# A recommender tower on one core: row transposes and MLP products at the array's full width, and part of ScalarE's copies one step sooner

## The chip, the cores and the metric

The kernel runs on one core of a Trainium2 chip. The metric is device time in microseconds (us), from the start of the program to the end of its last instruction. A change counts here as measurable when it is over 1% of the time, about 12 us.

TensorE is written PE in the profile, its weight loads PEld, VectorE DVE, ScalarE ACT, GpSimd POOL, and SyncE, which issues most plain DMAs, SP. On this kernel's float32 operands every matmul of the code appears in the trace as two records of MATMUL and two of LDWEIGHTS; a bfloat16 matmul appears as one of each. A record of MATMUL with its LDWEIGHTS is called a pair below.

## The reference

For a batch of 2048, 40 categorical fields are looked up in 40 tables with rows of 32 floats. Every pair of fields (780 pairs) gives one bilinear number; these and 16 dense values go through an MLP:

```python
e = jnp.stack([tbl_0[ids[:, 0]], ..., tbl_39[ids[:, 39]]], axis=1)      # (2048, 40, 32)
z = jnp.einsum('bpd,pde,bpe->bp', e[:, iidx, :], bilinear_matrices, e[:, jidx, :])   # (2048, 780)
h = jnp.concatenate([z, dense_ctx], axis=1)                             # (2048, 796)
h = jnp.maximum(h @ W_top1 + b_top1, 0.0)                               # 512 wide
h = jnp.maximum(h @ W_top2 + b_top2, 0.0)                               # 256 wide
y = h @ W_top3                                                          # (2048, 1)
```

## The kernel before

**Tiling.** The batch is cut into five blocks `o` of 256, 512, 512, 512 and 256 rows (`ROWS`). The 40 fields are ten chunks `J` of four fields, so that a chunk's vectors, transposed, fill 128 partitions (`x_T`, `x_look`: partition = field and dimension, column = batch row). A unit `(a, J)` stands for the field pairs between chunks a and J; 50 units cover everything. Where `a` is even, the unit `(a, a)` also takes the pairs inside chunk a + 1; it is the twin unit, and it needs the tile `x_twin`, a reordered mixture of chunk a + 1 and chunk a. Chunks are worked from 9 down to 0, so units are few at the start of a block and many (ten for chunk 0) at its end. A cycle `g` is one unit of 512 rows, or two units of 256 rows; there are 200 cycles: 25, 50, 50, 50 and 25.

**Where the vectors come from.** Seven fields (36 to 39, 0, 2, 3) are looked up on TensorE: VectorE compares indices (`one_hot`, L599) and TensorE multiplies ones with the table in three bfloat16 parts (`look`, L682). The other 33 fields are gathered by GpSimd: `DMA_INDIRECT` at L425, 128 rows each, 528 in all. A chunk's gathers go to one of 12 slots of `rows`. A turn (`turn`, L705) transposes a slot's rows: one matmul with the identity for each 128 rows and each field, which writes 32 partitions of a bank of `U`; ScalarE copies that bank to `x_T` (`keep_turn`, L467). Before GpSimd may fill the slots for turn n it waits for turn n - 12 (`turned`). Turns come in the order of chunks, so they are 2, 2, 4, 4, 6, 6, 8 cycles apart in a block of 512 rows.

**A cycle.** TensorE's program is one list written out by the loop at the end: `project(g + 1)` (L733, and L742 for a twin unit), which multiplies x with the bilinear matrices to `U`; then `sum_up(g - 1)` (L758), which adds VectorE's products over partitions into `bank_z`; then the cycle's parts of looks or of the MLP from the table `MISC_AT` (L682 or L788); then any turn. VectorE multiplies `U` by the other chunk (`multiply`, L617 to L635). ScalarE's list follows the same cycles: `keep_z` (L456), `keep_look`, `keep_mlp` (L503, L506), `keep_turn` (L467), then `copy_twin` (L491, L494, L496), seven copies in three lines, the last of which signals `twin_copied`; TensorE waits for it before a twin unit.

**The MLP.** A job `("mlp", o, j)` is one result tile of 128 rows of h1 (j = 0 to 3, seven parts t each), of h2 (j = 4, 5, four parts) or y (j = 6). A part before the change is four matmuls, each with 32 columns of weights, which fill the four quarters of one bank. The last block's MLP stands behind the loop: `sum_up(G - 1)`, then for each t the four j of h1, then h2 and y.

In the trace's names 128*32 stands for a weight tile of 128 partitions by 32 columns.

## Time and profile before

| what | value |
|---|---|
| median of 3 runs | 1256.24 us (1253.74 to 1262.59) |
| the profiled execution's own time | 1248.72 us |
| its span in the trace | 1247.1 us |
| mean granted clock of TensorE | 0.797 of full speed |
| TensorE busy, MATMUL records | 885.4 us (71%), 7918 |
| VectorE busy | 537.8 us (43%) |
| ScalarE busy | 176.0 us (14%) |
| GpSimd busy | 505.1 us (41%), 528 gathers of 955 ns |

The table is read so: TensorE is the busiest engine, but is idle or held up for over a quarter of the span, and most of that lies in the first two thirds. The profiled execution is 7.5 us below the median.

### The profile page before, as it was taken

The numbers are of one execution on the slowest core, as the hardware profiler recorded it, in microseconds if no ns is written. First come the engines' busy times: TensorE is split into PE (matmuls) and PEld (weight loads), VectorE is DVE, ScalarE is ACT, GpSimd is POOL, SyncE is SP. The second block draws the span as 40 slices with busy tenths as digits, with TensorE's granted clock in tenths as the row PEclk, the third lists the DMA queues.
The fourth block names the chain that finished last, engine by engine and source line by source line (L and its number), as shares of the span: only waits on it lengthen the run. The fifth ranks groups of instructions, "written<-read, shape, count | busy, mean of one in ns | idle before, by whom it ended". The sixth has DMA issues, their size and how long they took to land.

```text
span 1247.1 us, 18181 instructions
## 1 busy us (share of the span) xinstructions
PE 885.4 (71%) x7918; PEld 317.4 (25%) x7918; DVE 537.8 (43%) x601; ACT 176.0 (14%) x318; POOL 505.1 (41%) x535
## 2 busy tenths in 40 slices
PE   3110034668767668797897865699997889999998
PEld 2000011224322222222232221122223222324444
DVE  3000012226434233464475323276663558776652
ACT  2000111010101201020110210102112112024121
POOL 7777556662444565524431564612315430000000
PEclk8555555767767777797798777889997889999999
DMA  4200000361122100100010010000000000000000
GB/s 77 38 13 13 11 10 11 48 70 18 33 53 38 18 12 11 23 6 9 9 13 5 10 13 9 13 4 6 6 4 11 9 6 2 1 1 2 2 2 2
DMA packets 61280, 20.04 MB, mean 16 GB/s; under 512 B 46759, under 2 KB 60396, under 8 KB 61202
## 3 DMA queue, kind: packets, MB, share of 16 engines
q0 software_dynamic: 16896, 8.68, 5.2%
q1 hardware_dynamic: 44292, 10.18, 4.5%
q8 instruction: 62, 1.02, 0.3%
q14 instruction: 16, 0.13, 0.0%
q10 hardware_dynamic: 14, 0.03, 0.0%
HBM read 18.81 MB, written 0.04 MB: 15 GB/s over the span
## 4 chain that ended last, share of the span: by engine, by line
PE 61%; another core or an unknown queue 21%; issue 12%; ACT 4%; DVE 1%; DMA 0%; ACTq 0%; DVEq 0%
PE U L733 19%; PE bank_z L758 18%; PE misc L788 10%; PE misc L682 5%; PE U L705 4%; PE U L742 3%; ACT x_twin L491 1%; PE U L788 1%; DVE prod L635 1%; ACT x_twin L494 1%; ACT x_twin L496 0%; ACT x_T L467 0%; ACT z L456 0%; ACT W L529 0%
## 5 line engine op out<-in xcount | busy, mean ns | idle before, releaser
L425 POOL DMA_INDIRECT rows<-in_tbl,idx x528 | 504.3, 955 | 522.9 <-PE U L705 349.0
L635 DVE TENSOR_TENSOR prod<-U,x_T 128x1024 f32<-128x1024 f32 (+1 forms) x308 | 343.0, 1149 | 242.9 <-PE U L733 118.2
L733 PE MATMUL U<-x_T,W 32*128 32x512 f32 (+1 forms) x1440 | 245.7, 598 | 133.9 <-ACT x_twin L496 73.1
L758 PE MATMUL bank_z<-prod,select 128*32 128x512 f32 (+1 forms) x2000 | 272.6, 572 | 52.6 <-issue 40.7
L635 DVE TENSOR_TENSOR prod<-U,x_look 128x1024 f32<-128x1024 f32 (+1 forms) x90 | 89.1, 1007 | 240.1 <-PE U L742 101.0
L733 PEld LDWEIGHTS U<-x_T,W 32*128 32x128 f32 x1440 | 89.2, 201 | 263.1 <-issue 197.0
L682 PE MATMUL misc<-ones,tabs 125*32 125x512 bf16 (+1 forms) x1050 | 97.9, 390 | 61.0 <-issue 59.1
L788 PE MATMUL misc<-z,W 128*32 128x512 f32 (+1 forms) x952 | 117.1, 569 | 6.5 <-issue 5.5
L599 DVE TENSOR_SCALAR ones<-idx_wide,row_of 125x2048 bf16<-125x2048 f16 (+3 forms) x100 | 58.4, 606 | 134.3 <-remote 93.5
L705 PE MATMUL U<-ident,rows 128*32 128x128 f32 x1056 | 65.9, 305 | 68.8 <-issue 68.6
L758 PEld LDWEIGHTS bank_z<-prod,select 128*32 128x32 f32 x2000 | 53.4, 113 | 238.8 <-issue 167.0
L682 PEld LDWEIGHTS misc<-ones,tabs 125*32 125x32 bf16 x1050 | 42.5, 107 | 124.8 <-issue 109.3
L467 ACT ACTIVATE x_T<-U 128x512 f32<-128x512 f32 (+1 forms) x40 | 20.5, 512 | 378.6 <-PE U L705 325.5
L705 PEld LDWEIGHTS U<-ident,rows 128*32 128x32 f32 x1056 | 44.4, 123 | 106.1 <-issue 103.4
L733 PE MATMUL U<-x_look,W 32*128 32x512 f32 (+1 forms) x360 | 51.8, 565 | 3.7 <-issue 2.1
L456 ACT ACTIVATE z<-bank_z 128x512 f32<-128x512 f32 (+1 forms) x35 | 17.9, 512 | 254.9 <-remote 144.5
L788 PEld LDWEIGHTS misc<-z,W 128*32 128x32 f32 x952 | 33.6, 117 | 71.3 <-issue 63.7
L742 PE MATMUL U<-x_twin,W 32*64 32x512 f32 (+1 forms) x200 | 44.4, 604 | 2.1 <-issue 2.0
L788 PE MATMUL misc<-h,W 128*32 128x512 f32 (+3 forms) x272 | 39.7, 572 | 6.5 <-issue 3.1
L491 ACT ACTIVATE x_twin<-x_T 32x512 f32<-32x512 f32 (+1 forms) x80 | 43.4, 542 | 1.8
L742 PE MATMUL U<-x_T,W 32*64 32x512 f32 (+1 forms) x160 | 35.3, 605 | 3.9 <-ACT x_twin L496 3.0
L617 DVE TENSOR_TENSOR prod<-U,x_T 128x512 f32<-128x512 f32 (+1 forms) x20 | 11.6, 581 | 46.7 <-PE U L742 24.5
(64 smaller groups left out, 242.4 us busy)
## 6 DMA issues: line engine op xcount, KB each, us to landing
rows<-in_tbl,idx POOLq DMA_INDIRECT x528
idx_wide<-idx_rows SPq DMA_DIRECT2D x3, 500.0 KB
idx_wide<-idx_rows SPq DMA_DIRECT2D x3, 375.0 KB
W<-in_W_top SPq DMA_DIRECT2D x35, 2.0 KB
W<-_L_rec_bilinear_matrices SPq DMA_DIRECT2D x4, 128.0 KB
W<-in_W_top SPq DMA_DIRECT2D x1, 512.0 KB
W<-_L_rec_bilinear_matrices SPq DMA_DIRECT2D x30, 4.0 KB
W<-in_W_top SPq DMA_DIRECT2D x8, 56.0 KB
```

The lines of the kernel that those rows point to most:

```text
L425: nc.gpsimd.indirect_dma_start(out=rows[:, n % R_SLOTS, t, f, :], out_offset=None, in_=tables[field][:, :], in_offset=bass.IndirectOffsetO ...
L456: nc.scalar.activation(z[:, at % Z_SLOTS, 0:ROWS[o]], bank_z[:, 0:ROWS[o]], ACT.Copy).then_inc(z_kept, 1)
L467: nc.scalar.activation(x_of(o, J)[lo:hi, :], U[lo:hi, at, 0:N], ACT.Copy).then_inc(turn_kept, 1)
L491: nc.scalar.activation(x_twin[r * DIM:(r + 1) * DIM, 1, 0:N], x_of(o, a + 1)[(CF - 1 - r) * DIM:(CF - r) * DIM, :], ACT.Copy)
L599: nc.vector.tensor_scalar(ones[:, n % ONES, 0:len(fs), 0:N], idx_wide[q][:, :, 0:N], row_of[0:KP, k:k + 1], None, ALU.is_equal).then_inc(o ...
L635: last = nc.vector.tensor_tensor(to[:, :, m * N:(m + n) * N].rearrange("p r (m n) -> p r m n", m=n), U[:, at:at + 2, m * N:(m + n) * N].re ...
L682: last = nc.tensor.matmul(misc[f * DIM:(f + 1) * DIM, 0:N], tabs[0:KP, LOOKED.index(field), part, k * DIM:(k + 1) * DIM], ones[:, n % ONES ...
L705: last = nc.tensor.matmul(U[f * DIM:(f + 1) * DIM, at, t * P:(t + 1) * P], rows[:, n % R_SLOTS, t, f, :], ident[:], start=True, stop=True, ...
L733: last = nc.tensor.matmul(U[:, at + r % 2, m * N:(m + 1) * N], W[row, at_W:at_W + P], x_of(o, a)[row, :], start=True, stop=True, skip_grou ...
L742: last = nc.tensor.matmul(U[side * P // 2:(side + 1) * P // 2, at + r % 2, m * N:(m + 1) * N], W[row, at_W + side * P // 2:at_W + (side + ...
L758: last = nc.tensor.matmul(bank_z[r * DIM:(r + 1) * DIM, 0:N], sel, prod[:, (2 * g + r // 2) % P_SLOTS, r % 2, m * N:(m + 1) * N], start=(k ...
L788: last = nc.tensor.matmul(res, lhs, rhs, start=(t == 0), stop=(t == depth - 1), skip_group_check=True)
```

## The change

1. **Turns.** Where all four fields of a chunk are gathered (eight of the nine turns of a block), each 128 rows are turned by one `transpose` of 128x128 in place of four matmuls with 32 columns of weights. The turn of chunk 0, with one gathered field, is as before.
2. **MLP.** A part of h1 or h2 is one matmul with 128 columns of weights in place of four with 32. y is as before.
3. **ScalarE's copies.** `copy_twin` is cut in two. Six of its seven copies, which read chunk a + 1 alone, stand in ScalarE's list as soon as that chunk is there and the last twin unit has been multiplied (`TWIN_AT`); the seventh, which reads chunk a, stands where all seven stood (`mix_twin`, `MIX_AT`).
4. **Closing MLP.** Of the last block's h1, the six parts t < 6 of j = 0 come ahead of the last `sum_up`, then the six parts of j = 1, 2, 3, then the four last parts.

```diff
+    _mix = max(turn_cycle(_o, _a), TWIN_CYCLE[_n] - 3)
+    MIX_AT[_mix].append(_n)
+    TWIN_AT[min(_mix, max(turn_cycle(_o, _a + 1), TWIN_CYCLE[_n - 1] + 1 if _n else -2))].append(_n)
...
+            def mix_twin(n):
+                (o, a), N = TWINS[n], ROWS[TWINS[n][0]]
+                wait_kept(o, a)
                 nc.scalar.activation(x_twin[2 * DIM:, 0, 0:N], x_of(o, a)[2 * DIM:, :], ACT.Copy
                                      ).then_inc(twin_copied, 1)
...
                 for t in range(ROWS[o] // P):
-                    for f in GATHERED[c]:
-                        last = nc.tensor.matmul(U[f * DIM:(f + 1) * DIM, at, t * P:(t + 1) * P],
-                                                rows[:, n % R_SLOTS, t, f, :], ident[:], start=True, stop=True,
-                                                skip_group_check=True)
+                    if len(GATHERED[c]) == CF:
+                        last = nc.tensor.transpose(U[:, at, t * P:(t + 1) * P],
+                                                   rows[:, n % R_SLOTS, t].rearrange("p f d -> p (f d)"), ident[:])
+                    else:
...
-                for q in range(CF if j < RESULTS - 1 else 1):
-                    if j < H1 // P:
-                        lhs = W1[:, t, j * P + q * DIM:j * P + (q + 1) * DIM]
...
-                    res = bank[q * DIM:(q + 1) * DIM, 0:N] if j < RESULTS - 1 else bank[0:1, 0:N]
+                if j < H1 // P:
+                    lhs, rhs = W1[:, t, j * P:(j + 1) * P], z[:, (o * ZT + t) % Z_SLOTS, 0:N]
...
+                res = bank[:, 0:N] if j < RESULTS - 1 else bank[0:1, 0:N]
...
-            sum_up(G - 1)
             o, n = BLOCKS - 1, JOB[("mlp", BLOCKS - 1, 0)]
             pe.wait_ge(misc_kept, n)
-            for t in range(ZT):
-                for j in range(H1 // P):
-                    mlp(o, j, t, misc if j == 0 else U[:, j - 1, :])
+            for t in range(ZT - 1):
+                mlp(o, 0, t, misc)
+            sum_up(G - 1)
+            for j in range(1, H1 // P):
+                for t in range(ZT - 1):
+                    mlp(o, j, t, U[:, j - 1, :])
+            for j in range(H1 // P):
+                mlp(o, j, ZT - 1, misc if j == 0 else U[:, j - 1, :])
```

On TensorE, at the start of block 2 (a turn, a twin unit with the close of block 1's sums, and the first MLP parts), the program before reads (a row is an operation, its tiles, the output's size and the count of matmuls in the code):

```order
310 L705 MATMUL U<-ident,rows 32x128 x16
311 L742 MATMUL U<-x_T,W 64x512 x2
...
317 L758 MATMUL bank_z<-prod,select 32x512 x4
318 L766 MATMUL bank_z<-ident,dense 32x128 x16
319 L788 MATMUL misc<-z,W 32x512 x4
320 L733 MATMUL U<-x_T,W 128x512 x4
```

and after:

```order
310 L722 MATMUL U<-ident,rows 128x128 x4
311 L763 MATMUL U<-x_T,W 64x512 x2
...
317 L779 MATMUL bank_z<-prod,select 32x512 x4
318 L787 MATMUL bank_z<-ident,dense 32x128 x16
319 L806 MATMUL misc<-z,W 128x512
320 L754 MATMUL U<-x_T,W 128x512 x4
```

Nothing has moved there; sixteen instructions have become four, and four have become one.

On ScalarE, at the twin unit of chunk 0 in block 3, before (with the semaphores waited for; L467 is the copy behind chunk 0's turn):

```order
179 L503 ACTIVATE h1<-misc,b1 128x512 [waits mlp_full]
180 L467 ACTIVATE x_look<-U 32x512 [waits turned]
181 L491 ACTIVATE x_twin<-x_T 32x512 [waits misc_kept,turn_kept,multiplied]
182 L491 ACTIVATE x_twin<-x_T 32x512 x3
183 L494 ACTIVATE x_twin<-x_T 32x512 x2
184 L496 ACTIVATE x_twin<-x_look 64x512
```

and after:

```order
180 L501 ACTIVATE x_twin<-x_T 32x512 [waits turn_kept,multiplied]
181 L501 ACTIVATE x_twin<-x_T 32x512 x3
182 L504 ACTIVATE x_twin<-x_T 32x512 x2
183 L518 ACTIVATE h1<-misc,b1 128x512 [waits mlp_full]
184 L475 ACTIVATE x_look<-U 32x512 [waits turned]
185 L511 ACTIVATE x_twin<-x_look 64x512 [waits misc_kept,turn_kept]
```

Six copies have moved ahead of an MLP copy and of the turn's copy; one is left behind the turn.

On TensorE at the program's end, before:

```order
774 L758 MATMUL bank_z<-prod,select 32x256 x16
775 L766 MATMUL bank_z<-ident,dense 32x128 x8
776 L788 MATMUL misc<-z,W 32x256 x4
777 L788 MATMUL U<-z,W 32x256 x12
```

and after:

```order
774 L779 MATMUL bank_z<-prod,select 32x256 x8
775 L806 MATMUL misc<-z,W 128x256 x6
776 L779 MATMUL bank_z<-prod,select 32x256 x8
777 L787 MATMUL bank_z<-ident,dense 32x128 x8
778 L806 MATMUL U<-z,W 128x256 x18
779 L806 MATMUL misc<-z,W 128x256
780 L806 MATMUL U<-z,W 128x256 x3
```

Six MLP parts now stand between the last two sums; the rest of h1 follows them, result by result.

## Rows read from the trace of the kernel before

**Rows 1.** The page: busy time of each engine, and slices of GpSimd
```profile
PE 885.4 (71%) x7918; PEld 317.4 (25%) x7918; DVE 537.8 (43%) x601; ACT 176.0 (14%) x318; POOL 505.1 (41%) x535
...
POOL 7777556662444565524431564612315430000000
```

**Rows 2.** Windows, core 0: busy us and records of PE, PEld, DVE, ACT, POOL; clock
```profile
15.00:148.00 133.00, 15.29 (x78) 5.07 (x78) 3.99 (x11) 4.96 (x5) 100.79 (x106) 0.52 0.16 25
164.00:184.00 20.00, 8.13 (x64) 3.81 (x68) 3.97 (x7) 3.44 (x9) 15.34 (x16) 0.50 0.09 14
184.00:204.00 20.00, 5.12 (x28) 1.37 (x17) 1.29 (x2) 0.00 (x0) 15.14 (x16) 0.59 0.10 13
...
564.00:574.00 10.00, 9.21 (x90) 3.17 (x90) 5.48 (x6) 0.60 (x1) 7.56 (x8) 1.00 0.09 13
574.00:584.00 10.00, 4.77 (x15) 1.73 (x17) 1.23 (x1) 0.00 (x0) 7.57 (x8) 0.65 0.11 13
...
936.00:962.00 26.00, 19.46 (x149) 6.70 (x152) 9.40 (x9) 6.78 (x11) 15.14 (x16) 0.82 0.10 12
...
1056.00:1066.00 10.00, 10.00 (x84) 2.63 (x80) 8.04 (x8) 4.55 (x8) 0.00 (x0) 1.00 0.01 2
```

**Rows 3.** Timeline of POOL: first gather of a burst, and what ended its wait
```profile
690.29 0.95 POOL L425 DMA_INDIRECT rows<-in_tbl,idx  x1 [28.29 <-PE U L705]
...
738.14 0.94 POOL L425 DMA_INDIRECT rows<-in_tbl,idx  x1 [5.17 <-PE U L705]
...
792.58 0.95 POOL L425 DMA_INDIRECT rows<-in_tbl,idx  x1 [3.73 <-PE U L705]
825.50 0.95 POOL L425 DMA_INDIRECT rows<-in_tbl,idx  x1 [13.20 <-PE U L705]
```

**Rows 4.** Waits in all: us, times, longest us
```profile
POOL rows L425 <- PE U L705: 349.0, 29, 28.3
PE U L742 <- ACT x_twin L496: 11.7, 5, 3.8
```

**Rows 5.** Timeline of PE in block 3, no gathers under way
```profile
1087.11 1.14 PE L733 MATMUL U<-x_T,W 32*128 32x512 f32 x8
1088.18 1.07 PE L758 MATMUL bank_z<-prod,select 128*32 128x512 f32 x8
1089.06 1.04 PE L788 MATMUL misc<-h,W 128*32 128x512 f32 x8
1089.93 1.04 PE L705 MATMUL U<-ident,rows 128*32 128x128 f32 x8
```

**Rows 6.** Timeline of PE: a full turn of 512 rows; two MLP parts
```profile
562.91 1.05 PE L705 MATMUL U<-ident,rows 128*32 128x128 f32 x32
...
1145.63 1.90 PE L788 MATMUL misc<-z,W 128*32 128x512 f32 x16
1147.35 0.62 PE L705 MATMUL U<-ident,rows 128*32 128x128 f32 x16
```

**Rows 7.** Timeline of ACT and PE at the twin unit of chunk 0, block 3
```profile
1091.00 0.59 ACT L467 ACTIVATE x_look<-U 32x512 f32<-32x512 f32 x1 [8.50 <-PE U L705]
1091.67 2.54 ACT L491 ACTIVATE x_twin<-x_T 32x512 f32<-32x512 f32 x4
...
1095.50 0.63 ACT L496 ACTIVATE x_twin<-x_look 64x512 f32<-64x512 f32 x1
...
1096.38 0.65 PE L742 MATMUL U<-x_look,W 32*64 32x512 f32 x2 [2.49 <-ACT x_twin L496]
```

**Rows 8.** The chain that ended last, a turn inside a burst of gathers: start, us
```profile
730.84 0.21 PE U L705 x2
...
736.00 1.86 PE U L705 x26
```

**Rows 9.** Timeline at the start: ACT and POOL
```profile
138.55 0.38 ACT L476 ACTIVATE x_look<-misc 128x256 f32<-128x256 f32 x1 [123.85 <-remote]
...
163.78 0.38 ACT L467 ACTIVATE x_T<-U 128x256 f32<-128x256 f32 x1 [20.27 <-remote]
```

More of the change, by code:

```diff
@@ L198, with turn_cycle @@
 TWIN_AT = {g: [] for g in range(-2, G)}
+MIX_AT = {g: [] for g in range(-2, G)}
+def turn_cycle(o, J):
+    return next((g for g in TURN_AT if (o, CHUNK_OF_STEP.index(J)) in TURN_AT[g]), -2)
 for _n, (_o, _a) in enumerate(TWINS):
-    _turned = next(g for g in TURN_AT if (_o, CHUNK_OF_STEP.index(_a)) in TURN_AT[g])
-    TWIN_AT[max(_turned, TWIN_CYCLE[_n] - 3)].append(_n)
+    _mix = max(turn_cycle(_o, _a), TWIN_CYCLE[_n] - 3)
+    MIX_AT[_mix].append(_n)
+    TWIN_AT[min(_mix, max(turn_cycle(_o, _a + 1), TWIN_CYCLE[_n - 1] + 1 if _n else -2))].append(_n)
 U_SLOTS = 3
@@ L477, in keep_look, with wait_kept @@
                 last.then_inc(misc_kept, 1)
+            def wait_kept(o, J):
+                c = CHUNK_OF_STEP.index(J)
+                if GATHERED[c]:
+                    act.wait_ge(turn_kept, TURN[(o, c)] + 1)
+                if c in GROUP_OF_STEP:
+                    act.wait_ge(misc_kept, JOB[("look", o, GROUP_OF_STEP[c])] + 1)
             def copy_twin(n):
                 (o, a), N = TWINS[n], ROWS[TWINS[n][0]]
-                c = CHUNK_OF_STEP.index(a)
                 if n:
                     act.wait_ge(multiplied, 2 * (TWIN_CYCLE[n - 1] + 1))
-                for J in (a, a + 1):
-                    if GATHERED[CHUNK_OF_STEP.index(J)]:
-                        act.wait_ge(turn_kept, TURN[(o, CHUNK_OF_STEP.index(J))] + 1)
-                    if CHUNK_OF_STEP.index(J) in GROUP_OF_STEP:
-                        act.wait_ge(misc_kept, JOB[("look", o, GROUP_OF_STEP[CHUNK_OF_STEP.index(J)])] + 1)
+                wait_kept(o, a + 1)
                 for r in range(CF):
@@ L550, in _ @@
                     copy_twin(n)
+                for n in MIX_AT[g]:
+                    mix_twin(n)
             for j in range(RESULTS):
@@ L703, in turn @@
                 for t in range(ROWS[o] // P):
-                    for f in GATHERED[c]:
-                        last = nc.tensor.matmul(U[f * DIM:(f + 1) * DIM, at, t * P:(t + 1) * P],
-                                                rows[:, n % R_SLOTS, t, f, :], ident[:], start=True, stop=True,
-                                                skip_group_check=True)
+                    if len(GATHERED[c]) == CF:
+                        last = nc.tensor.transpose(U[:, at, t * P:(t + 1) * P],
+                                                   rows[:, n % R_SLOTS, t].rearrange("p f d -> p (f d)"), ident[:])
+                    else:
+                        for f in GATHERED[c]:
+                            last = nc.tensor.matmul(U[f * DIM:(f + 1) * DIM, at, t * P:(t + 1) * P],
+                                                    rows[:, n % R_SLOTS, t, f, :], ident[:], start=True, stop=True,
+                                                    skip_group_check=True)
                 last.then_inc(turned, 1)
@@ L776, in mlp @@
                     pe.wait_ge(z_kept, o * ZT + t + 1)
-                for q in range(CF if j < RESULTS - 1 else 1):
-                    if j < H1 // P:
-                        lhs = W1[:, t, j * P + q * DIM:j * P + (q + 1) * DIM]
-                        rhs = z[:, (o * ZT + t) % Z_SLOTS, 0:N]
-                    elif j < RESULTS - 1:
-                        m = j - H1 // P
-                        lhs = W2[:, t, m * P + q * DIM:m * P + (q + 1) * DIM]
-                        rhs = h1[:, t, 0:N]
-                    else:
-                        lhs, rhs = W3[:, t:t + 1], h2[:, t, 0:N]
-                    res = bank[q * DIM:(q + 1) * DIM, 0:N] if j < RESULTS - 1 else bank[0:1, 0:N]
-                    last = nc.tensor.matmul(res, lhs, rhs, start=(t == 0), stop=(t == depth - 1),
-                                            skip_group_check=True)
+                if j < H1 // P:
+                    lhs, rhs = W1[:, t, j * P:(j + 1) * P], z[:, (o * ZT + t) % Z_SLOTS, 0:N]
+                elif j < RESULTS - 1:
+                    m = j - H1 // P
+                    lhs, rhs = W2[:, t, m * P:(m + 1) * P], h1[:, t, 0:N]
+                else:
+                    lhs, rhs = W3[:, t:t + 1], h2[:, t, 0:N]
+                res = bank[:, 0:N] if j < RESULTS - 1 else bank[0:1, 0:N]
+                last = nc.tensor.matmul(res, lhs, rhs, start=(t == 0), stop=(t == depth - 1), skip_group_check=True)
                 if t == depth - 1:
```

## The prediction

> **What bounds the kernel now.** The page first: TensorE is busy for 71% of the span with 7918 pairs, GpSimd for 41% [rows 1]. GpSimd's slices show that its gathers run until about 1030 us, and the reader should see that they come in bursts. So I read TensorE in windows laid over those bursts. In 10 us without a gather TensorE passes 84 pairs; in the first 10 us of a burst 90, in the second 10 us of the same burst 15, with nothing but "issue" before them [rows 2]. Over a longer burst it is worse: 64 pairs in the first 20 us from 164 us on, 28 in the next 20, and 78 in the 133 us from 15 to 148 us [rows 2]. Something about a running burst holds TensorE up, after a number of pairs that varies much less than their time does. I call these stretches the crawl; the rows don't tell its cause. It seems to go by instructions: in a crawl a turn of 32 pairs takes from 730.8 to 737.9 us, where it takes 1.05 us otherwise [rows 6, 8].
>
> A burst ends when GpSimd meets a slot whose turn has not run: that wait is 349.0 us in all [rows 4], and it is also what lets TensorE recover. Turn n starts gathers of turn n + 12; so the two engines hand each other the time. GpSimd's own work, 528 gathers at 8 in 10 us [rows 2], is 660 us and isn't changed.
>
> From about 825 us on the bursts are short and the kernel is bound by TensorE: project 1.07 us, sum 0.88, MLP part 0.87, one behind the other [rows 5], while VectorE is busy for 8.04 of 10 us [rows 2].
>
> **Twin copies.** At chunk 0 the turn is followed by seven copies, 1091.67 to 1096.13 us, and TensorE starves for 2.49 us at the twin unit [rows 7]; there are 5 such waits with 11.7 us [rows 4]. Only the 0.59 us copy of the turn and the 0.63 us seventh copy stay behind the turn, so 3.8 us leave that path, about the longest of the five waits. At the startup twin both halves keep their place, so nothing is gained there. The six copies now queue ahead of an MLP copy; they wait for `multiplied` of a cycle whose sum ScalarE's next z copy awaits anyway, and what stands behind them on ScalarE is late by 3.8 us at most, with the MLP's next job behind it. That takes back some. Between -12 and 0; I take **-10**.
>
> **Turns, where TensorE runs freely.** 32 pairs take 1.05 us [rows 6]; these are four column tiles working side by side, so each of the eight passes of a tile takes about 0.12 us. The same follows from chunk 0's turn, whose 8 pairs in one tile take 1.04 us [rows 5]. No row shows a 128x128 transpose. If it still takes two passes, a turn of 512 rows is 8 passes one behind another, about 1 us, and nothing is gained; if it takes one, 0.5. Twenty-four turns of 512 rows and sixteen of 256 are changed: at the lower end 24 x 0.5 + 16 x 0.25 = 16 us less, at the other 0. Cycles that VectorE bounds hide some of it; I take **-12**, near the one-pass end, since a transpose moves data and need not be split like a product.
>
> **MLP parts, where TensorE runs freely.** Two parts of 512 rows take 1.72 us from 1145.63 to 1147.35 [rows 6], 0.86 each: 8 pairs in four tiles at once, so two passes of 0.43 us. One matmul of 128 columns also needs two passes over 512 columns, 0.86 us. So the streaming gives nothing back; fewer instructions do nothing here. What is new is a change of the array's shape between sum (32 columns wide) and part (full). Rows: project, whose shape differs from its neighbours', takes 1.07 us to the next start, the sum with the same four matmuls 0.88 [rows 5]. A change so costs 0 to 0.2 us, and 114 cycles hold a changed part: 0 to +23. I take 0.1 each, **+12**.
>
> The Trainium skill, TensorEngine Tiling, Key Properties, speaks against the change here: changing the tiling mode, and not just the tile, drains the engine. It gives no time; the 0.2 us above is the only price there is, and with it the sum would be 12 us higher.
>
> **Thinner instruction stream in the crawl.** A cycle of 512 rows is 8 + 8 + 8 pairs with an MLP part and becomes 18; a turn is 32 and becomes 4 or 8. Looks (9 or 12 pairs a part) stay, and fill most cycles until 435 us, and again from 489 to 710. If a burst passes about 90 pairs whatever they are, the work of a burst grows only where MLP parts and turns fall into it. Taken burst by burst from GpSimd's restarts [rows 3]:
> - 690.3 to 738.1 us (two turns, each two cycles behind the last): 73 + 120 pairs become 45 + 80. The first turn now ends within 7 us, so GpSimd doesn't stop: its 40 us run on to 730, the second 20 with hardly any progress, and the last 30 pairs need the time until about 738. Gain 0: the two bursts have joined.
> - 738.1 to 792.6: 120 + 128 pairs become 74 + 82; the same join, then rest: 788, gain 5.
> - 792.6 to 825.5: 168 become 110. 90 pass in the 22 us of the burst, 20 more at 8.4 a us: 25 us instead of 33, gain 8.
> - 458 to 690 us, five bursts filled mostly with looks: about 3.5 us in each of the two that hold MLP parts at their start, 7.
> - 850 to 990 us, bursts of 10 us, some of which meet: 936 to 962 us holds 149 pairs where 218 would pass at the free rate [rows 2], 8 us lost. Two or three such places, most of it given back: 10.
>
> Together **-30**; -5 if the crawl goes by time alone, -90 if joined bursts still passed 90 pairs per 20 us (below).
>
> **Startup and block 0.** The chain's 120 look pairs are done at 138.5 us, turn 0 at 163.8 [rows 9]: 16 pairs in 25 us, of which 2 or 4 remain, 14 to 20 us sooner. But GpSimd's first burst ends at 148 us; with turn 0 done by then it doesn't stop, and project(0), 24 pairs, falls into the crawl until turn 12's gathers end at 168 and TensorE has recovered (15 us after the first burst). Turn 1 then comes at about 187 in place of 181, turn 2 sooner (its burst no longer joined), turn 3 about where it was. I take **0**, between -15 and +20.
>
> **The close.** TensorE fills a gap of half a microsecond before the last sum; 36 parts stream as before. **-1**.
>
> **Sum.** -10 - 12 + 12 - 30 + 0 - 1 = -41: 1248.7 becomes about 1208 us for the profiled execution. The median lies 7.5 us above that execution; with the same distance the forecast is **1215 us**.
>
> **The rivals.**
> *The crawl admits pairs, not time, even in joined bursts.* Then the 23 full bursts each carry 90 of pairs that are 30% richer (7918 pairs become about 6000, 25% fewer, for nearly the same work): 23 x 90 x 0.3 / 8.4 = 74 us in place of 30, and startup gives its 15. 1215 - 44 - 15 = 1156 us. For it: the first halves of bursts. Against: 28 pairs in the second 20 us from 184 on, 78 in 133 us [rows 2]. 18%.
> *The crawl doesn't care for instructions, or full-width passes cost more.* Copies and turns gain 22, the crawl 5, and shape changes take 23: 1256 - 4 = 1252 us, no measurable change. 15%.
> *Joined bursts: slower.* Turns get done early, GpSimd never stops, and TensorE crawls for 40 us and more. A join costs the 90 pairs that a fresh burst would have passed less those it does pass; at 28 that is 62 pairs, 7 us. It can happen at startup, and at three places in each of blocks 1 and 2, where turns are two cycles apart: 7 x 7 = 49 us, where my sum counts them as quits. With the thinning reduced to 15 for it: 1215 + 49 + 15 = 1279 us. It decides if a join passes fewer than 30 pairs. Against it: GpSimd's work is finite, and a join moves its waits, which are 349 us [rows 4], to later, where there are no bursts. 10%.
> *The forecast itself*, 57%.
>
> **How the numbers follow.** My own case spans 1180 to 1240 us by the ends of its terms. The range of 8 in 10 runs from 1155, which takes in the large gain, to 1252, which takes in the case of no change. Measurement tells 1% or 12.6 us from no change: faster by more than that 0.77, within it 0.13, slower 0.10.
>
> **What would show it.** Turn records fall from 1056 to about 160 or 290 (one pass or two), MLP records by some 1080; waits on the seventh copy at a twin unit fall from 11.7 us to under 2. MLP cycles from 1030 to 1226 us stay at 2.9 to 3.0 us. Windows over bursts hold about 90 pairs, and more sums. GpSimd's restarts between 690 and 825 come less often but not sooner on the whole. The prediction is wrong if the crawl vanishes or lengthens, or if a full-width part takes over 1.1 us where it took 0.86.

## The result, and the profile of the kernel after

After: 1239.26 us median of 19 runs (1233.35 to 1253.81); before, on the same chips: 1256.78 us (1249.62 to 1264.24). The ratio is 0.987, 95% interval 0.985 to 0.990: some 17 us less, just over the 1% that counts here, where the forecast had 41 us less. Here and in the table below medians are of all runs, while ratios leave out the runs of a slower state (one of after's 19 here; two of e14's four). The profiled execution of after took 1244.90 us, its span is 1243.3 us, the mean granted clock 0.783.

The two profiled executions lie only 3.8 us apart (1248.72 and 1244.90): the one of before is faster than its median, the one of after slower. So the two traces can show what a burst or a cycle costs, but not where the whole 17 us lie.

The page of after: busy time of the engines, and slices of GpSimd.

```profile
PE 878.8 (71%) x5942; PEld 306.9 (25%) x5942; DVE 539.2 (43%) x601; ACT 175.5 (14%) x318; POOL 505.8 (41%) x535
...
POOL 7777647462445566514432646522224430000000
```

Against [rows 1], 1976 pairs are gone and TensorE's busy time is 6.6 us shorter: a quarter of the instructions was hardly any of the work.

Waits in all in after (us, times, longest); L722 and L726 are the turns (full, and chunk 0), L763 the twin unit, L754 a project.

```profile
POOL rows L433 <- PE U L722: 280.3, 22, 27.6
...
PE U L754 <- ACT x_twin L511: 92.1, 1, 92.1
...
POOL rows L433 <- PE U L726: 53.0, 3, 20.5
...
PE U L763 <- ACT x_twin L511: 1.2, 1, 1.2
```

GpSimd waits for turns 333 us where it waited 349, and the five waits at twin units with 11.7 us [rows 4] have become one with 1.2. The wait of 92.1 us is the startup's and no new one; before has it at L733 with 71.8 us.

Windows of after, columns as in [rows 2]: the startup burst, a joined burst in block 0, a joined burst at 690 us, a stretch without gathers.

```profile
15.00:148.00 133.00, 12.09 (x72) 3.71 (x65) 4.21 (x12) 1.93 (x5) 100.86 (x106) 0.51 0.16 25
...
186.30:206.30 20.00, 13.20 (x92) 5.57 (x92) 11.45 (x18) 4.56 (x11) 15.39 (x16) 0.67 0.09 14
206.30:226.70 20.40, 6.37 (x11) 1.92 (x12) 0.00 (x0) 0.00 (x0) 15.48 (x17) 0.50 0.09 13
...
688.60:708.60 20.00, 13.01 (x85) 3.66 (x81) 6.45 (x7) 2.90 (x6) 15.10 (x17) 0.73 0.08 12
708.60:728.30 19.70, 3.16 (x9) 1.15 (x9) 1.23 (x1) 0.00 (x0) 15.09 (x16) 0.50 0.09 13
1056.00:1066.00 10.00, 10.00 (x74) 2.89 (x74) 7.13 (x7) 0.60 (x1) 0.00 (x0) 1.00 0.01 2
```

The crawl is unchanged: some 80 to 90 pairs at the front of a burst, then almost nothing. Bursts join at 186 and at 690 us, as forecast, and at 941 us. The join forecast at 738 us didn't come: GpSimd waited 3.3 us at 764.22.

GpSimd's restarts in after, to set beside [rows 3].

```profile
688.62 0.94 POOL L433 DMA_INDIRECT rows<-in_tbl,idx  x1 [27.53 <-PE U L722]
...
741.26 0.94 POOL L433 DMA_INDIRECT rows<-in_tbl,idx  x1 [13.00 <-PE U L722]
...
764.22 0.94 POOL L433 DMA_INDIRECT rows<-in_tbl,idx  x1 [3.31 <-remote]
...
792.29 0.94 POOL L433 DMA_INDIRECT rows<-in_tbl,idx  x1 [8.40 <-PE U L722]
826.91 0.94 POOL L433 DMA_INDIRECT rows<-in_tbl,idx  x1 [14.94 <-PE U L722]
```

This is the reading that matters. 690.29, 738.14, 792.58 and 825.50 us of before are 688.62, 741.26, 792.29 and 826.91: where the forecast had TensorE gain 13 us from 690 to 825 us, it has lost 3. Other traces with the crawl, from several chips, bear that out. Times between the starts of the same gathers (numbered from 0; the last column is from gather 510 to the end of the span), in us:

| trace | 378 to 458 (690 to 825 us in before) | 442 to 458 (the last burst of these) | 262 to 378 | 462 to 510 | 510 to the end |
|---|---|---|---|---|---|
| before | 135.2 | 32.9 | 255.5 | 140.8 | 262.2 |
| e7, before's code but for the start | 135.1 | 33.8 | 265.6 | 140.7 | 262.7 |
| e8, turns alone | 139.1 | 33.5 | 265.1 | 139.7 | 262.7 |
| e13, copies alone | 139.0 | 33.6 | 263.8 | 140.9 | 253.6 |
| e9, MLP alone | 134.9 | 34.8 | 256.0 | 135.3 | 271.1 |
| after | 138.3 | 34.6 | 255.5 | 138.8 | 258.8 |

From 378 to 458 no thinner stream gains anything; in the last of these bursts the two kernels with the 128-wide MLP parts are 1 to 2 us slower than the four others, where 8 us were to be won. From 262 to 378 (about 435 to 690 us) the same code differs by 10 us between before and e7, so single traces settle nothing there.

### What one burst does with the thinner stream

Both kernels start a burst at 792 us; the last gather is issued at 811. TensorE in after, then in before.

```profile
801.95 1.99 PE L754 MATMUL U<-x_T,W 32*128 32x512 f32 x8
803.88 1.06 PE L779 MATMUL bank_z<-prod,select 128*32 128x512 f32 x8
805.65 1.13 PE L754 MATMUL U<-x_T,W 32*128 32x512 f32 x4 [0.71 <-issue]
816.19 2.07 PE L754 MATMUL U<-x_T,W 32*128 32x512 f32 x4 [9.41 <-DVE prod L652]
818.19 1.94 PE L779 MATMUL bank_z<-prod,select 128*32 128x512 f32 x8
820.06 2.08 PE L806 MATMUL misc<-z,W 128*128 128x512 f32 x2
822.07 2.08 PE L754 MATMUL U<-x_T,W 32*128 32x512 f32 x8
824.08 1.06 PE L779 MATMUL bank_z<-prod,select 128*32 128x512 f32 x8
```

```profile
805.10 1.12 PE L733 MATMUL U<-x_T,W 32*128 32x512 f32 x2
806.65 1.01 PE L733 MATMUL U<-x_T,W 32*128 32x512 f32 x2 [0.43 <-issue]
813.69 2.08 PE L733 MATMUL U<-x_T,W 32*128 32x512 f32 x4 [6.03 <-issue]
815.70 1.94 PE L758 MATMUL bank_z<-prod,select 128*32 128x512 f32 x8
817.56 1.98 PE L733 MATMUL U<-x_T,W 32*128 32x512 f32 x8
819.47 1.06 PE L758 MATMUL bank_z<-prod,select 128*32 128x512 f32 x8
```

Both stall at 806 us in the middle of a project, but after is one project and one sum further on: behind the stall it has one more project until the turn, before has two. Priced by rows at the free rate, that lead is worth about 1.5 us (6.1 us of work up to the turn instead of 7.7). Then after comes out of the stall at 816.2 instead of 813.7, and four of its groups instead of three take about twice their time (2.08 against 1.14 us for a whole project): they run at the lower of the clock's two levels, 1.2 GHz (granted clock 0.50 from 816.2 to 824.0 us, 0.51 from 813.7 to 819.4 us in before), after 9.41 us of idle time where before had 6.03. They lose 3.7 us by it, before's three 2.8. So 2.5 and 0.9 us are lost against 1.5 won, and the turn starts 1.9 us later (826.03 for 824.14).

The stall is not TensorE's alone. VectorE in after, then in before:

```profile
814.91 4.70 DVE L652 TENSOR_TENSOR prod<-U,x_T 128x1024 f32<-128x1024 f32 x4 [9.32 <-remote]
```

```profile
812.41 1.23 DVE L635 TENSOR_TENSOR prod<-U,x_T 128x1024 f32<-128x1024 f32 x1 [11.49 <-remote]
```

In after VectorE sat idle for 9.32 us, though the last matmul of the half project that it multiplies had begun at 802.49 us; TensorE's 9.41 us are a wait for VectorE in turn. In before that matmul began at 800.10 us and the multiplication at 812.41. In free cycles it follows after about 1 us. So inside the crawl TensorE's work is also made known late, or finished late (the ends of matmuls are modelled), and the forecast's "nothing but issue" is half of the picture. In e3's trace, which has no crawl, VectorE sits idle for over 1 us beyond that first microsecond at 2 of its 400 multiplications; in after's trace at 42.

### A cycle that nothing disturbs

TensorE in after, block 3.

```profile
1081.29 1.13 PE L806 MATMUL misc<-h,W 128*128 128x512 f32 x2
1082.35 1.14 PE L754 MATMUL U<-x_T,W 32*128 32x512 f32 x8
1083.42 1.06 PE L779 MATMUL bank_z<-prod,select 128*32 128x512 f32 x8
1084.41 1.12 PE L806 MATMUL misc<-h,W 128*128 128x512 f32 x2
```

And in before, the part ahead of [rows 5]:

```profile
1086.14 1.04 PE L788 MATMUL misc<-h,W 128*32 128x512 f32 x8
```

From part to part 3.12 us, in before 2.92. In before the sum is followed after 0.88 us [rows 5], here after 0.99, and the part after 1.06 where one with 32 columns takes 0.97 to the next project (1087.11). So it is 0.1 us at each of the two borders, 0.2 us a cycle: the forecast had charged 0.1 a cycle.

### The profile page after: what moved, and what is told of

Its sections match the earlier page's. It is cut to its first block, busy times and chain, and to the rows that moved or that the text cites. A ratio compares the mean times of both kernels' runs of the same rounds, so it can differ in the third digit from the quotient of the medians.

```text
span 1243.3 us, 14228 instructions
## 1 busy us (share of the span) xinstructions
PE 878.8 (71%) x5942; PEld 306.9 (25%) x5942; DVE 539.2 (43%) x601; ACT 175.5 (14%) x318; POOL 505.8 (41%) x535
## 4 chain that ended last, share of the span: by engine, by line
PE 58%; another core or an unknown queue 27%; issue 10%; ACT 3%; DVE 1%; DMA 0%; ACTq 0%; DVEq 0%
PE U L754 18%; PE bank_z L779 17%; PE misc L806 11%; PE misc L699 6%; PE U L763 3%; PE bank_z L787 1%; PE U L722 1%; PE U L806 1%; DVE prod L652 1%; ACT x_twin L501 1%; ACT x_T L475 0%; ACT z L464 0%; PE U L726 0%; ACT x_twin L504 0%
## 5 line engine op out<-in xcount | busy, mean ns | idle before, releaser
L754 PE MATMUL U<-x_T,W 32*128 32x512 f32 (+1 forms) x1440 | 238.2, 599 | 166.6 <-ACT x_twin L511 92.1
L779 PE MATMUL bank_z<-prod,select 128*32 128x512 f32 (+1 forms) x2000 | 264.9, 568 | 42.5 <-issue 24.9
L754 PEld LDWEIGHTS U<-x_T,W 32*128 32x128 f32 x1440 | 88.2, 202 | 285.4 <-issue 208.9
L699 PE MATMUL misc<-ones,tabs 125*32 125x512 bf16 (+1 forms) x1050 | 107.9, 401 | 66.8 <-issue 64.0
L806 PE MATMUL misc<-z,W 128*128 128x512 f32 (+1 forms) x238 | 121.4, 612 | 3.4 <-ACT h L518 3.4
L806 PEld LDWEIGHTS misc<-z,W 128*128 128x128 f32 x238 | 40.5, 202 | 82.3 <-issue 75.9
L754 PE MATMUL U<-x_look,W 32*128 32x512 f32 (+1 forms) x360 | 52.6, 574 | 3.9 <-DVE prod L652 3.6
L763 PE MATMUL U<-x_T,W 32*64 32x512 f32 (+1 forms) x160 | 40.0, 634 | 14.0 <-DVE prod L652 10.3
L806 PE MATMUL misc<-h,W 128*128 128x512 f32 (+3 forms) x80 | 39.9, 593 | 8.0 <-ACT x_look L482 6.4
L787 PE MATMUL bank_z<-ident,dense 128*32 128x128 f32 x128 | 18.3, 332 | 35.6 <-issue 35.6
L763 PE MATMUL U<-x_twin,W 32*64 32x512 f32 (+1 forms) x200 | 40.8, 614 | 1.0 <-issue 0.9
L640 DVE TENSOR_TENSOR prod<-U,x_twin 128x1024 f32<-128x1024 f32 (+1 forms) x25 | 25.1, 1004 | 21.9 <-remote 21.9
L722 PE MATMUL U<-ident,rows 128*128 128x128 f32 x128 | 24.5, 298 | 9.8 <-issue 9.7
```

Source lines behind the costliest of these rows:

```text
L640: last = nc.vector.tensor_tensor(to[:, :, m * N:(m + 1) * N], U[:, at:at + 2, m * N:(m + 1) * N], x_twin[:, :, 0:N], ALU.mult)
L699: last = nc.tensor.matmul(misc[f * DIM:(f + 1) * DIM, 0:N], tabs[0:KP, LOOKED.index(field), part, k * DIM:(k + 1) * DIM], ones[:, n % ONES ...
L722: last = nc.tensor.transpose(U[:, at, t * P:(t + 1) * P], rows[:, n % R_SLOTS, t].rearrange("p f d -> p (f d)"), ident[:])
L754: last = nc.tensor.matmul(U[:, at + r % 2, m * N:(m + 1) * N], W[row, at_W:at_W + P], x_of(o, a)[row, :], start=True, stop=True, skip_grou ...
L763: last = nc.tensor.matmul(U[side * P // 2:(side + 1) * P // 2, at + r % 2, m * N:(m + 1) * N], W[row, at_W + side * P // 2:at_W + (side + ...
L779: last = nc.tensor.matmul(bank_z[r * DIM:(r + 1) * DIM, 0:N], sel, prod[:, (2 * g + r // 2) % P_SLOTS, r % 2, m * N:(m + 1) * N], start=(k ...
```

## Experiments

The same kernel has two conditions that no text of it chooses. The kernel before took 1256 to 1274 us in three of the five sets of runs, as in the recorded result, and **774 us in the two others**; within a set it was always the same, and one chip (number 6) showed 774 in the first set and 1274 ten minutes later. The forecast was made for the slow one. Each kernel is compared with before in its own set.

| run | kernel | before, us | this, us | ratio (95% interval) |
|---|---|---|---|---|
| e1 | turns alone | 773.7 | 772.9 | 0.999 (0.998 to 1.000) |
| e2 | MLP alone | 773.7 | 782.5 | 1.013 (1.011 to 1.015) |
| e3 | copies alone | 773.7 | 768.4 | 0.993 (0.991 to 0.995) |
| e4 | after without the MLP's part | 773.7 | 766.3 | 0.991 (0.989 to 0.993) |
| e5 | after | 1273.7 | 1251.9 | 0.980 (0.975 to 0.986) |
| e6 | before, pause after 8 gathers | 1273.7 | 1185.9 | 0.929 (0.924 to 0.935) |
| e7 | before, pause for the first look | 1273.7 | 1267.9 | 0.997 (0.994 to 1.000) |
| e8 | turns alone | 1256.2 | 1261.5 | 1.001 (0.998 to 1.004) |
| e9 | MLP alone | 1256.2 | 1257.3 | 1.001 (0.998 to 1.005) |
| e10 | after, pause after 8 | 1256.2 | 1114.5 | 0.886 (0.880 to 0.891) |
| e11 | e4's kernel, pause after 8 | 1256.2 | 1118.1 | 0.887 (0.882 to 0.892) |
| e12 | before, probes on GpSimd | 1270.7 | 1300.0 | one run |
| e13 | copies alone | 1270.7 | 1263.5 | 0.994 (0.991 to 0.997) |
| e14 | after, pause after 6 | 1270.7 | 945.6 | 0.735 (0.728 to 0.741) |
| e15 | after, pause after 4 | 1270.7 | 957.9 | 0.755 (0.751 to 0.758) |
| e16 | before, pause after 6 | 774.0 | 895.7 | 1.157 (1.154 to 1.159) |
| e17 | e4's kernel, pause after 6 | 774.0 | 888.5 | 1.147 (1.145 to 1.149) |
| e18 | e4's kernel, pause after 5 | 774.0 | 906.0 | 1.172 (1.169 to 1.176) |

### The parts alone (e1 to e4)

Each is the kernel before with one hunk of the change's diff: e1 `nc.tensor.transpose` in `turn`, e2 the single matmul in `mlp`, e3 `mix_twin` and its table; e4 has all but e2's.

> The kernel before with the 128x128 transposes alone. In the kernel after, a turn of 512 rows takes some 0.5 us where it took 1.05, and turns 3 to 26 end within a few us of where they ended before. Theory (the gain of the turns lies only where TensorE runs freely, and GpSimd's bursts swallow the rest): about 6 to 16 us faster than before, 1240 to 1250 us. Rival (the thinner stream helps within a burst, and the MLP's change took it back): 25 us or more, 1230 or less.

> The kernel before with the MLP parts as 128x128 matmuls alone. The trace of after shows an MLP cycle at 3.12 us where it was 2.93, that is 0.2 us for each of 114 cycles, 81 of them past 900 us. Theory (two changes of the array's shape cost 0.1 us each, and nothing in the bursts pays for it): 10 to 20 us slower than before, 1266 to 1276 us. Rival, the recorded forecast's terms: 12 us for the shapes, less the MLP's share of the thinner stream, some 15 us: no change, 1253. A third: the 0.2 us belong to the turns' and copies' side of the change, and this kernel is within 3 us of before with cycles at 2.93.

> The kernel before with ScalarE's six copies made sooner, alone. Waits of TensorE on x_twin outside of the startup fell from 11.7 to 1.2 us in after. Theory: 5 to 10 us faster, 1246 to 1251 us. Rival (the work behind a twin unit only waits for VectorE instead): within 3 us of before.

> The kernel after with the MLP parts as in before (32 columns of weights): transposes, copies and the closing order stay. Theory (the MLP's part of the change costs 10 to 20 us): 1220 to 1230 us, faster than after's 1239. Rival (thinner MLP parts help in the bursts as much as they cost elsewhere): 1237 to 1241, as after.

No crawl was there. The page of e3, busy times and slices of TensorE and GpSimd:

```profile
PE 688.5 (90%) x7918; PEld 269.2 (35%) x7918; DVE 532.8 (69%) x601; ACT 175.7 (23%) x318; POOL 510.1 (67%) x535
...
PE   4579999677799999986999999996999999999998
...
POOL 7777777777777777777777777777777777700000
```

GpSimd gathers in one burst from 3 to 672 us, TensorE is 90% busy beside it with the same 7918 pairs, and nobody slows anybody. So the bound is different: GpSimd's list until 672 us, TensorE's 95 us after it. In that regime the parts read cleanly. The MLP costs 8.8 us, and all of it falls in the last 50 cycles, at 0.2 us each (49 x 0.2 = 10); at 610 us e1 and e2 are level within 1 us. The copies give 5.3 us. The turns give 0.8, within the noise. e4's 7.4 is the copies', the turns' and about one for the close. The theory for e3 held; e2 cost a little less than the 10 to 20 us expected, and for e1 less came than the 6 to 16 us, since GpSimd hides what is won before 672 us. All four were meant for the condition with the crawl, so for it they say nothing yet.

### After again, and a pause between gathers (e5 to e7)

e6 and all later kernels with a pause:

```diff
+            issued, left = [0] * R_SLOTS, 8
             for n, (o, c) in enumerate(TURNS):
...
                         ).then_inc(gathered[n % R_SLOTS], 16)
+                        issued[n % R_SLOTS] += 1
+                        left -= 1
+                        if left == 0:
+                            pool.wait_ge(gathered[n % R_SLOTS], 16 * issued[n % R_SLOTS])
+                            left = 8
```

e7 has `if n == 1: pool.wait_ge(ones_used, KC)` there instead.

> The kernel after, unchanged, beside before on the chip of this call. On the chip of the first four comparisons before took 773.7 us and had no crawl: GpSimd gathered without a stop to 672 us and TensorE was never held up. If this call's chip is like that one: the parts there were -0.8 (turns), -5.3 (copies), +8.8 (MLP), and -7.4 for all but the MLP; theory, they add up: +1 to +3 us, 774 to 777. Rival (the closing order and the faster turns hide part of the MLP's cost): 770 or less. If it is like the chip of the recorded result (before near 1256 us): 0.987 of before again.

> The kernel before, with GpSimd waiting after every eighth gather until those of that slot have landed, about 2.5 us: 66 pauses. Theory (the crawl is made by an unbroken run of gathers, and a short pause ends it): on a chip where before takes some 1256 us, 850 to 1000 us. Rival (the crawl goes by the number of gathers or by something else on that chip): 1250 us or more. On a chip where before takes 774 us there is nothing to cure and GpSimd is the bound: 66 pauses of 2.3 us cost 100 to 155 us, 875 to 930 us.

> The kernel before, with GpSimd waiting after turn 0's eight gathers until TensorE has done the first look (ten parts). Theory, on a chip with the crawl: the look takes 20 us in place of 125, the remaining 106 gathers run from about 40 to 172 us, beside work of block 0 instead of the look: 30 to 100 us faster than 1256. Rival (the crawl falls on block 0's cycles instead): within 12 us. On a chip without the crawl the gathers are GpSimd's bound and all come some 20 us later: 790 to 800 us.

e5 repeats the result and is, at 0.980 (0.975 to 0.986), a little better. e6 took 88 us off a kernel by making GpSimd wait: the pause theory is right in sign and too bold in size (850 to 1000 us were expected, 1186 came). e7 fits its rival: the copy behind turn 0 began at 23 us in place of 164, but the 138 gathers behind the look still ran in one burst, from 18 to 190 us, and the copy behind turn 2 began at 212 us where before has 210. The burst has to be broken, not moved.

### The parts with the crawl (e8, e9, e13)

> The transposes alone again, for the condition with the crawl (before at 1256 to 1274 us). Before against after by the ends of the turns showed no gain up to 900 us, though a turn of 512 rows has 8 pairs in place of 32. Theory (the bursts swallow the thinner stream; some 6 us come from turns past 900 us): 0.990 to 0.998 of before. Rival (the transposes do thin the crawl and the MLP's change hid it): 0.98 or less. In the condition without the crawl (before at 774 us): 0.999 again.

> The 128-wide MLP parts alone again, for the condition with the crawl. Without the crawl they cost 0.2 us in each cycle of the last 50, where TensorE is the bound, and nothing before, where GpSimd is. With the crawl TensorE is the bound in 81 such cycles from about 900 us on: theory, 16 us, and 6 parts' worth fewer records in the bursts of blocks 1 and 2 give back 0 to 10: 1.005 to 1.013 of before. Rival, the recorded forecast (12 us for shapes, 15 us back from the thinner stream): 0.998. In the condition without the crawl: 1.013 again.

> ScalarE's six copies made sooner, alone, for the condition with the crawl (before 1256 us). Turns alone and MLP alone gave 1.001 each there, and all together 0.980 to 0.987. Theory (the copies carry most of the gain): 0.985 to 0.993. Rival (the parts gain only together, as when turns and copies move in the same bursts): 0.997 to 1.003. Without the crawl: 0.993 again.

Alone, turns and MLP are each worth nothing (1.001), the copies 8 us (4 to 12). e8 so missed both of its texts (0.998 at most was expected), e9 came out between its theory and its rival, and e13 at the edge of its theory. Three parts make 5 us less, give or take about 7 by their intervals; the whole change made 16 us less by the recorded ratio and 25 by e5's. The rest, 10 to 20 us, comes only in combination or from the closing order, which was not tried alone; for the latter the traces show nothing (from the z copy to the end 20.6 us in after, 20.7 in before). These are different sets of runs, so some of the rest can be a difference between sets.

Within the MLP's 1.5 us two things cancel. From gather 510 to the end, where the bursts are nearly over, e9's trace is 8.9 us longer than before's (271.1 for 262.2, table above): the borders' price. From 462 to 510 it is 5.5 us shorter (135.3 for 140.8): there the thinner MLP parts do gain.

Why the turns give nothing even late, e8's TensorE at a turn of 256 rows between two MLP parts and a project:

```profile
1159.13 1.90 PE L792 MATMUL misc<-z,W 128*32 128x512 f32 x16
1160.96 0.44 PE L705 MATMUL U<-ident,rows 128*128 128x128 f32 x2
1161.33 1.16 PE L737 MATMUL U<-x_T,W 32*128 32x256 f32 x16
```

and before's project behind the same turn as in [rows 6]:

```profile
1147.90 1.16 PE L733 MATMUL U<-x_T,W 32*128 32x256 f32 x16
```

The turn is 0.37 us long instead of 0.55, but the parts ahead of it take 1.83 instead of 1.72: changing the array's shape costs the transposes 0.11 us too, and 0.07 is left. A turn of 512 rows takes 0.59 us, with the same 0.1 ahead of it, and some of what remains is spent waiting for VectorE.

### Thinner stream and pauses together (e10, e11)

> The kernel after with GpSimd's pause after every eighth gather, as in e6_land8 (which took 0.929 of before). Theory (a thinner stream pays once bursts don't join, because what a pause restores is a number of records): 0.89 to 0.91. Rival (records don't count at all, time does): 0.929 less the 1.3 to 2% that after gains: 0.91 to 0.92; second rival (the MLP's shapes cost more than that): 0.93 or more. Without the crawl (before 774 us): 1.12 to 1.20.

> The same with the MLP parts as in before. Theory (MLP's shapes cost 16 us past 900 us and give back less than 10 us in the bursts): 5 to 15 us faster than e10, 0.885 to 0.905. Rival (the thinner MLP parts pay in blocks 1 and 2): as e10 or slower. Without the crawl (before 774 us): as e10 less 0.01.

e10 came out a little better than its theory. With pauses the change is worth 4.4 points (0.929 to 0.886, from two sets of runs) where it is worth 1.3 to 2.0 without. The likely reason is that the thinner stream pays once the bursts don't join; no run has it alone under pauses. e11 came out against its theory, which had it 5 to 15 us faster than e10. Where nothing disturbs them the MLP's shapes cost 10 us in the last 50 cycles alone; here the two kernels are equal, so the thinner MLP parts earn that back in the bursts. This is an inference from two totals; no run separates it.

### What makes the crawl (e12)

```diff
+            pool.wait_ge(summed, 138)
+            for i in range(24):
+                nc.gpsimd.memset(spare[:, 0:1024], 0.0).then_inc(worked, 1)
+                pool.wait_ge(worked, i + 1)
+            pool.wait_ge(summed, 155)
+            for i in range(16):
+                pool.dma_start(spare[...], tables[...][...]).then_inc(probed, 16)
+            pool.wait_ge(summed, 170)
+            for i in range(24):
+                nc.gpsimd.indirect_dma_start(out=spare[...], ...).then_inc(probed, 16)
```

> The kernel before, with extra work for GpSimd in the last quarter, where no gathers of its own are left and TensorE runs freely (84 pairs in 10 us): from the 138th sum on 24 memsets of 128x1024 one by one, from the 155th on 16 plain DMAs of 16 KB, from the 170th on 24 indirect gathers back to back. The extra results aren't used. Theory (the descriptors or the transfers of indirect gathers make the crawl, not GpSimd's being busy): TensorE passes 80 or more pairs per 10 us beside the memsets and the plain DMAs, and beside the gathers about 80 in the first 10 us and under 40 in the next 15. Rival (a busy GpSimd is enough): under 40 pairs per 10 us already beside the memsets, from 10 us on. Third (the late stretch is free of it for another reason): over 80 everywhere. Without the crawl (before at 774 us) all three are over 80.

Windows over the memsets, the plain DMAs, the first, second and third 10 us of gathers, and the 10 us from 2.5 us behind them:

```profile
1053.20:1063.20 10.00, 10.00 (x80) 2.69 (x80) 8.11 (x8) 1.14 (x2) 9.48 (x10) 1.00 0.04 3
1063.20:1073.20 10.00, 10.00 (x108) 3.39 (x104) 7.99 (x7) 0.60 (x1) 9.43 (x11) 1.00 0.01 2
...
1094.80:1103.40 8.60, 8.60 (x72) 2.33 (x70) 7.28 (x7) 0.60 (x1) 8.55 (x16) 1.00 0.15 30
...
1141.50:1151.50 10.00, 9.17 (x76) 2.54 (x68) 5.63 (x5) 1.27 (x2) 7.67 (x8) 1.00 0.09 13
1151.50:1161.50 10.00, 1.08 (x16) 0.59 (x16) 0.00 (x0) 2.40 (x6) 7.56 (x8) 0.66 0.09 14
1161.50:1171.50 10.00, 1.48 (x5) 0.71 (x5) 1.22 (x1) 0.87 (x3) 7.57 (x8) 0.50 0.09 13
1174.00:1184.00 10.00, 9.14 (x78) 3.83 (x81) 4.89 (x8) 1.26 (x3) 0.00 (x0) 0.60 0.01 2
```

The theory holds, in the one run that was made. A GpSimd busy for 24 us with memsets takes nothing from TensorE (80 and 108 pairs in 10 us). Gathers put where there never were any bring it nearly to a stop within the second 10 us: 76, 16, 5 pairs. Whether it is their descriptors, their transfers or their landings that do it, this run doesn't tell. The plain DMAs prove nothing: all 16 were issued in 8.6 us, and a burst of gathers of that length does no harm either.

### Shorter bursts (e14, e15)

The same edit with 6 and with 4 in place of 8.

> The kernel after with GpSimd's pause after every sixth gather in place of every eighth (e10, 0.886 of before): 88 pauses. Theory (a burst of 6 ends before TensorE's credit of records does, and 2.8 us restore it): GpSimd's list takes 528 x 1.25 + 88 x 2.8 = 906 us when nothing else holds it, TensorE follows, and the rest after the last gather is 100 us: 1000 to 1060 us, 0.80 to 0.85. Rival (more pauses only cost): 1120 us or more, 0.89. Without the crawl: 1.20 to 1.32 of before's 774.

> The same with a pause after every fourth gather, 132 pauses: GpSimd's list takes 660 + 370 = 1030 us, plus 100. Theory (no crawl at all, GpSimd is the bound): 1110 to 1140 us, 0.88 to 0.91, TensorE's rate near 80 pairs per 10 us where it has work. Rival (the crawl stays at the same share whatever the pauses): 1180 or more. Without the crawl: 1.4 to 1.5 of 774.

e14 is 325 us faster than before (its four runs spread from 927 to 959 us) and far better than even its theory's 1000. A pause is shorter than assumed: six gathers and a wait take 8.9 us (starts at 305.26 and 314.19), so GpSimd's list is 88 x 8.9 = 783 us. GpSimd's waits in e10, e14 and e15:

```profile
POOL rows L434 <- DMA rows<-in_tbl,idx: 117.6, 64, 4.6
POOL rows L434 <- PE U L728: 103.9, 9, 19.3
```

```profile
POOL rows L434 <- DMA rows<-in_tbl,idx: 157.4, 85, 4.9
...
POOL rows L434 <- PE U L728: 1.7, 1, 1.7
```

```profile
POOL rows L434 <- DMA rows<-in_tbl,idx: 248.9, 131, 5.4
```

At eight GpSimd still waits for a crawling TensorE for 104 us at full turns; at six and at four it waits for hardly more than its own pauses. And TensorE from 300 to 400 us in e10, e14 and e15 passes 285, 650 and 804 pairs:

```profile
300.00:400.00 100.00, 64.69 (x285) 20.20 (x281) 24.91 (x25) 8.49 (x15) 66.28 (x71) 0.73 0.08 12
```

```profile
300.00:400.00 100.00, 85.97 (x650) 30.38 (x653) 65.10 (x70) 15.12 (x26) 64.19 (x68) 0.95 0.09 13
```

```profile
300.00:400.00 100.00, 92.71 (x804) 33.60 (x804) 80.42 (x90) 18.55 (x32) 58.46 (x62) 0.97 0.09 13
```

e15's last gather starts at 877.6 us and the span ends 76 us later, so it is bound by GpSimd's list alone, as its theory said (its time was put too high for the same reason as e14's). e14's last gather is at 803.2 and the end 146 us later: TensorE is some 70 us behind, with a remainder of the crawl.

### What the change is worth under pauses (e16 to e18)

> The kernel before with GpSimd's pause after every sixth gather; e14, the kernel after with it, took 0.735 of before, and the pair e6 and e10 at every eighth 0.929 and 0.886. In 7.5 us TensorE passes 63 pairs of before's stream (84 in 10 us), the 57 to 95 at which the crawl set in. Theory (what a burst admits is a number of records, so the thicker stream runs into the crawl sooner): 0.76 to 0.82, slower than e14 by 3 points or more. Rival (a burst of 6 is short enough for any stream; the change gives its 5 us of copies and no more): 0.735 to 0.745. Without the crawl (before 774): 1.13 to 1.17.

> Transposes, copies and closing order, MLP parts as in before, a pause after every sixth gather. Theory (with the crawl nearly gone the MLP's 0.2 us a cycle stand alone, in 50 to 80 cycles): 10 to 16 us faster than e14, 0.72 to 0.73. Rival (the thinner MLP parts still buy bursts without a crawl): 0.735 or more. Without the crawl: 1.12 to 1.16.

> The same with a pause after every fifth gather: GpSimd's list is 106 x (4 x 1.25 + 2.65) = 811 us, plus 100 us behind it and some 10 ahead: 920. At six it is 88 x 8.9 = 783, at which 945 us were measured, 50 above its bound; at four 840 and 958, right at its bound. Theory (at five hardly any crawl is left and GpSimd is the bound): 915 to 935 us, 0.72 to 0.735, as e17 within 1%. Rival (crawl left at five as at six): 945 or more. Without the crawl: 1.17 to 1.20.

These fell in the condition without the crawl, so their question, whether a burst of six admits the thicker stream, stays open; so does how much of e14's gain is the pauses' and how much the change's. They show the price of the cure where there is nothing to cure: 1.157 for six, and e18 costs 18 us over e17, as GpSimd's list grows (the 28 us worked out from 783 and 811 were too many). e17 is 7 us below e16, which is e4's gain again.

The best version depends on the condition. With the crawl it is e14 (945.6 us, 0.735); without it e4 (766.3 us, 0.991).

## Why the prediction came out as it did

**Right:** the sign; the bound (the crawl beside GpSimd's bursts); that bursts would join at 186 and at 690 us; one pass for a transpose (160 turn records in all instead of 1056; a full turn takes 0.53 to 0.59 us instead of 1.05); and that the startup would give back what turn 0 wins: the copy behind turn 0 came 11 us sooner, behind turn 1 5 us later, turn 2 15 us sooner, turn 3 3 us later. In e5's trace of the same kernel turn 0 won nothing (168.7 us), and turn 3 came at 241.4.

**Twin copies, -10:** -8 us (4 to 12) alone. Right; e13's trace has 8.6 us of it behind gather 510.

**Thinner stream, -30:** this is the step that failed, at "738.1 to 792.6: gain 5" and "792.6 to 825.5: gain 8": from 690 to 825 us 13 us were expected, and no trace has more than 0.3. At 792.6 I had 90 pairs pass in the 22 us of the burst and priced the 20 left at 8.4 a us, 2.4 us. The trace above shows TensorE coming back after 24 us with 36 pairs left to the turn's end and not 20; they are worth 6.1 us up to the turn and not 2.4, since the thinned pairs carry more work each (18 of them take 3.12 us, 5.8 a us); and the clock at half adds 3.7. With 0.9 for the turn itself that makes 34.6 us from burst to burst where 25 were forecast and before had 32.9. From 850 to 990 us, where 10 us more were expected, after gains 2.0 and e9 5.5 (gather 462 to 510). The 7 us between 458 and 690 can't be told from single traces.

The other extreme, that joined bursts make the kernel slower, had its condition fulfilled (fewer than 30 pairs in a join: 11 and 9 in the windows above) and still lost: after joins three bursts, not seven.

**Turns, -12:** with e8 at +1 us (-2 to +5), at least 10 us too much, and their share of the thinner stream is in that number too. The transposes are as fast as hoped; I had left out the border that they bring themselves, 0.11 us ahead of each, and taken every turn as if it lay on the path.

**MLP shapes, +12:** where nothing disturbs them 0.2 us a cycle, not 0.1. The Trainium skill, TensorEngine Tiling (Array Packing), Key Properties, says that changing the tiling mode drains the engine; the traces agree, with 0.1 us a border. At 0.2 us the 81 late cycles would pay about 16 us, an estimate; e9's trace shows 8.9 us behind gather 510. In all e9 is +1.5 us (-3 to +6), so the thinner MLP parts gave back some 7 us ahead of that.

**The close, -1:** nothing in the traces.

**The sum.** By the recorded ratio the change made 16 us less. With the copies at -8 and the shapes at about +9, turns and thinner stream together have -17, where the forecast had -42; by e5's ratio they have -26. How this splits between them is not shown: alone in e8 and e9 they give less, and the two profiled executions of before and after don't hold the difference. What the traces do show is that the stretch from 690 to 825 us has no part of it. That the result lay within the range is owed to the range's taking in the case of no change.

**Open:** what puts a chip or a session in the crawl's condition; what resource gathers take from TensorE there; the 10 to 20 us that only the whole change has. One candidate can be set aside for the stall above, late instruction code: in before no packet of an instruction queue moved from 800 to 821 us, while TensorE came back at 813.7. Another was not tried: every run on record comes with the profiler's span and clock, so whether recording has a part in the crawl is not known.

## What to carry to other kernels

A stall that ends by itself has an after-effect: work that it holds back didn't run at the free rate when it ended, so don't price it so, and count that work in time and not in instructions. When two engines disturb each other in bursts, try to break the burst before you thin the stream: here a wait of under 2 us after every eighth gather was worth four times the change studied, and after every sixth, with the change, 325 us. One trace of each kernel is not enough to place a gain of 1%: here the same code differed by 10 us in one stretch. And before tuning to a stall, measure on another chip and at another time: here the same kernel also ran in 774 us, without it, and there the pauses cost 15%.

## What the runs showed of the hardware

- The same kernel takes 774 or about 1260 us, on one chip even, by whether TensorE crawls beside indirect gathers from GpSimd. GpSimd's own pace is the same, 1.25 us a gather, in both.
- In the crawl's condition TensorE passes 76 pairs in the first 10 us of gathers, then 16, then 5 (e12); memsets on GpSimd do nothing to it. With a pause of about 1.7 us of idle time after every sixth or fourth gather it passes 650 or 804 pairs in 100 us (e14, e15), after every eighth 285 (e10).
- In the crawl VectorE too starts late on TensorE's results: 12 us after the matmuls began in before and in after at 792 us, where it is about 1 us in free cycles.
- Behind a stall of 6 to 9 us of idle time TensorE's next 6 to 8 us had a granted clock of 0.5.
- A change between 128x32 tiles and the full array costs 0.1 us between neighbouring float32 matmuls, measured at three borders: sum to part, part to project, part to transpose.
- A float32 transpose of 128x128 is one MATMUL record, a float32 matmul two.
